# A grouped-norm and depthwise-convolution kernel: coefficients by block copies instead of a matrix product, and the last images' projections, copies and x-additions at other places

## The reference

```python
x = x + conv(gn(x), w1, w3, w5, w_proj)            # x: (8, 32, 64, 64) float32
# gn: 32 groups of one channel: each channel of each image is normalised over its 64 x 64 pixels
# conv:
xd = concatenate([x[:, :, 0::2, 0::2], x[:, :, 0::2, 1::2],
                  x[:, :, 1::2, 0::2], x[:, :, 1::2, 1::2]], axis=1)      # (8, 128, 32, 32)
feats = concatenate([dwconv(xd, w1, 1), dwconv(xd, w3, 3), dwconv(xd, w5, 5)], axis=1)
y = einsum('bchw,oc->bohw', feats, w_proj)          # 384 -> 128 channels, back to 32 x 64 x 64
```

## Time and profile before

| | us |
|---|---|
| median of 3 runs (135.26 to 136.7) | 135.5 |
| the profiled execution | 135.7 |
| its span, first to last instruction | 133.9 |
| TensorE clock granted, mean over the span | 0.986 of full |
| PE / DVE / POOL / ACT busy | 124.9 / 125.0 / 119.9 / 110.3 |

### The profile page before, as it was taken

One profiled execution on the slowest core, in us unless ns is written; L12 is line 12 of the kernel. 1 busy time (PEld: TensorE's weight loads), 2 busy tenths in 40 slices (PEclk: granted clock), 3 DMA queues, 4 the chain that ended last, 5 costly groups with the idle time before them and its releaser, 6 DMA issues.

```text
span 133.9 us, 1668 instructions
## 1 busy us (share of the span) xinstructions
PE 124.9 (93%) x514; PEld 96.8 (72%) x514; DVE 125.0 (93%) x234; ACT 110.3 (82%) x116; POOL 119.9 (90%) x92
## 2 busy tenths in 40 slices
PE   6968999999999999999999999999999999999910
PEld 6955788888886887688886888688877688578700
DVE  6679999999979999999999999999999999999960
ACT  2389979999999999999999999999999999160010
POOL 6269879999999999999999999999999999999970
PEclk9999999999999999999999999999999999999995
DMA  4999999880044008097979873989299919897876
GB/s 136 260 250 201 207 209 201 169 167 0 5 81 81 0 0 161 5 117 95 187 115 117 155 168 39 91 144 190 30 100 134 186 37 115 91 110 145 182 159 143
DMA packets 35944, 16.68 MB, mean 125 GB/s; under 512 B 34144, under 2 KB 34272, under 8 KB 35552
## 3 DMA queue, kind: packets, MB, share of 16 engines
q0 software_dynamic: 1488, 6.93, 38.8%
q1 hardware_dynamic: 32784, 9.11, 35.6%
q10 hardware_dynamic: 1664, 0.54, 1.7%
HBM read 5.46 MB, written 4.19 MB: 72 GB/s over the span
## 4 chain that ended last, share of the span: by engine, by line
POOL 62%; issue 16%; DVE 12%; PE 4%; POOLq 1%; ACT 1%; ACTq 0%
POOL RING_SUM L343 56%; DVE ACC L649 4%; POOL X L393 3%; PE YP L691 3%; POOL LO L330 2%; DVE st L546 2%; DVE weff L600 2%; DVE whi L608 1%; POOLq L102 1%; DVE ACC L645 1%; DVE stp L552 1%; DVE HI L623 1%; PE YP L795 1%; POOL rstd L312 0%; POOL wlo L385 0%
## 5 line engine op out<-in xcount | busy, mean ns | idle before, releaser
L343 POOL TENSOR_TENSOR RING_SUM<-RING_SUM,PROD 128x900 f32<-128x900 f32 (+1 forms) x45 | 93.0, 2072 | 3.4
L649 DVE SCALAR_TENSOR_TENSOR ACC<-G,coef,ACC 128x480 f32<-128x480 f32 (+3 forms) x132 | 82.4, 742 | 0.0
L476 ACT ACTIVATE PROD<-G,coef 128x900 f32<-128x900 f32 (+1 forms) x45 | 44.5, 1051 | 0.0
L723 PE MATMUL YP<-HI,wlo 128*128 128x512 f32 (+1 forms) x146 | 38.1, 412 | 0.0
L723 PE MATMUL YP<-HI,whi 128*128 128x512 f32 (+1 forms) x146 | 36.2, 398 | 1.7 <-DVE HI L623 1.2
L723 PE MATMUL YP<-LO,whi 128*128 128x512 f32 (+1 forms) x146 | 36.0, 398 | 0.0
L723 PEld LDWEIGHTS YP<-HI,wlo 128*128 128x128 f32 x146 | 27.5, 189 | 8.6 <-issue 2.9
L723 PEld LDWEIGHTS YP<-HI,whi 128*128 128x128 f32 x146 | 27.2, 189 | 8.7 <-DVE HI L623 1.3
L723 PEld LDWEIGHTS YP<-LO,whi 128*128 128x128 f32 x146 | 27.5, 189 | 6.7 <-issue 0.5
L438 ACT ACTIVATE G<-X,nbias,rstd 64x1024 f32<-64x1024 f32 x16 | 21.1, 1321 | 1.2 <-DVE nbias L564 0.9
L459 ACT ACTIVATE Y<-YP 64x1024 f32<-64x1024 f32 x14 | 15.4, 1097 | 3.4 <-PE YP L778 3.1
(11 more groups left out here) (69 smaller groups left out, 66.4 us busy)
## 6 DMA issues: line engine op xcount, KB each, us to landing
LO<-G POOLq DMA_DIRECT2D x7, 527.5 KB, 5.3
X<-in_x_dram SPq DMA_DIRECT2D x14, 256.0 KB, 5.5
X<-Y POOLq DMA_DIRECT2D x6, 512.0 KB, 7.3
out_dram<-X SPq DMA_DIRECT2D x12, 256.0 KB, 4.5
XS<-in_x_dram SPq DMA_DIRECT2D x1, 512.0 KB, 6.1
out_dram<-X SPq DMA_DIRECT2D x4, 128.0 KB, 2.2
X<-in_x_dram SPq DMA_DIRECT2D x2, 136.0 KB, 4.4
XS<-in_x_dram SPq DMA_DIRECT2D x1, 256.0 KB, 3.3
```

The lines of the kernel that those rows point to most:

```text
L343: pool.tensor_tensor(dst, dst, prod(b, k), ALU.add).then_inc(prod_added, 1)
L476: act.activation(prod(b, k), g_tap(b, POOL_OF[b][k + 1]), ACT.Copy, scale=of5(POOL_OF[b][k + 1])).then_inc(prod_ready, 1)
L649: dve.scalar_tensor_tensor(half_part(ACC, tap, h), half_tap(b, tap, h), of5(tap), half_part(ACC, tap, h), ALU.mult, ALU.add).then_inc(acc_ ...
L723: mm = nc.tensor.matmul(dst, w[:, n, :], src, start=start, stop=False, skip_group_check=True)
```

## The change

Three things at the start. The coefficients are no longer made on PE: four copies of 32 partitions each bring `w_sb` into the ph order, for w5 and w3 on DVE and for w1 on POOL, each with a semaphore of its own (`coef5`, `coef3`, `coef1`). The third part of w_proj is transposed first, ahead of the statistics' sum, into another bank and with its own count. And ACT starts seven of the weff, without a break, POOL two; PE's first row of warm matmuls has 17 for 20.

At the other end, the ring of image 4 is projected behind `low(5)`, Y of images 4 and 5 is copied inside images 6 and 7 (before products 4 and 3), the x-addition of image 4 is issued inside image 6, and x of the upper half of image 6 is added by a DMA (behind POOL's sum (7, 5)) in place of a POOL instruction. Of the lower half's two stores one is issued by ACT.

```diff
@@ -48,11 +48,11 @@
 TOP = BANK_ROWS + 1
-WARM = (20, 5)
+WARM = (17, 5)
 WARM_COLS = 256
...
 CHUNKS = N_INNER // CHUNK
-ACT_SCALED = 5
+ACT_SCALED = 7
 PARTS = 4
@@ -61,10 +61,13 @@
 AREAS = 3
-ADD_X_AT = {(b + AREAS, 0): b for b in range(B - AREAS)}
+ADD_X_AT = {(b + AREAS, 0): b for b in range(4)}
+ADD_X_AT[(6, 3)] = 4
 ADD_X_AT[(7, 1)] = 5
-COPY_Y_AT = {(7, 4): 5}
-RING_AFTER_HIGH = {2: 0, 3: 1, 4: 2, 5: 3, 6: 4, 7: 6}
+ADD_TOP6_AT = (7, 5)
+COPY_Y_AT = {(6, 4): 4, (7, 3): 5}
+RING_AFTER_HIGH = {2: 0, 3: 1, 4: 2, 5: 3, 7: 6}
+RING_AFTER_LOW = {5: 4}
 COMBINE_AT = {(0, 8): (1, 1, 2), (1, 1): (2, 2, PAIRS)}
...
@@ -244,6 +246,11 @@
+
+        def in_order(c0, c1, block):
+
+            src = (block % 2) * 2 + block // 2
+            return coef[C * block:C * (block + 1), c0:c1], w_sb[C * src:C * (src + 1), c0:c1]
@@ -269,9 +276,10 @@
                 store(b, 0, PH)
-            for half in range(2):
-                sp.wait_ge(half_added, half + 1)
-                store(B - 2, half * BANK_ROWS, (half + 1) * BANK_ROWS)
+            sp.wait_ge(row_added[B - 2], 16)
+            store(B - 2, 0, BANK_ROWS)
+            sp.wait_ge(half_added, 1)
+            store_rows(sp, B - 2, 0, BANK_ROWS, PH)
             for n, (r0, r1) in enumerate(LAST_ROWS):
@@ -343,28 +351,39 @@
                         add_x(ADD_X_AT[b, k])
+                    if (b, k) == ADD_TOP6_AT:
+                        add_x(B - 2, BANK_ROWS)
                     if (b, k) in INV_STD_AT:
...
-            def add_x(b):
+            def add_x(b, rows=PH):
...
                 pool.wait_ge(y_copied, 2 * (b + 1))
-                pool.dma_start(X[p0:p0 + HALF, t, :, :].rearrange("p h w -> p (h w)"),
-                               Y[p0:p0 + HALF, t % 2, :, :, :].rearrange("p h w j -> p (h w j)"),
+                pool.dma_start(X[p0:p0 + HALF, t, 0:rows, :].rearrange("p h w -> p (h w)"),
+                               Y[p0:p0 + HALF, t % 2, 0:rows, :, :].rearrange("p h w j -> p (h w j)"),
                                accum_op=ALU.add).then_inc(row_added[b], 16)
...
+            pool.wait_ge(wpT_ready, 1)
+            pool.wait_ge(coef5, 4)
+            scale_w5(ACT_SCALED)
             inv_std(1, 0, 1)
-            pool.wait_ge(wpT_ready, 1)
-            pool.wait_ge(coef_copied, 1)
-            scale_w5(ACT_SCALED)
             pool.wait_ge(weff_step, CHUNK)
...
                 scale_w5(n)
+            pool.wait_ge(w1_loaded, 16)
+            for block in range(PARTS):
+                if block == 0:
+                    pool.wait_ge(pool_scaled, N_INNER - ACT_SCALED)
+                else:
+                    pool.wait_ge(coef1, block)
+                to, of = in_order(W1_AT, N_COEF, block)
+                pool.tensor_copy(to, of).then_inc(coef1, 1)
+            pool.wait_ge(coef1, PARTS)
             for k in range(CHUNKS):
@@ -386,11 +405,9 @@
             pool.wait_ge(y_copied, 2 * (B - 1))
-            for half in range(2):
-                rows = slice(half * BANK_ROWS, (half + 1) * BANK_ROWS)
-                xr = X[0:HALF, PAIRS - 1, rows, :].rearrange("p h w -> p (h w)")
-                yr = Y[0:HALF, (PAIRS - 1) % 2, rows, :, :].rearrange("p h w j -> p (h w j)")
-                pool.tensor_tensor(xr, xr, yr, ALU.add).then_inc(half_added, 1)
+            xr = X[0:HALF, PAIRS - 1, BANK_ROWS:PH, :].rearrange("p h w -> p (h w)")
+            yr = Y[0:HALF, (PAIRS - 1) % 2, BANK_ROWS:PH, :, :].rearrange("p h w j -> p (h w j)")
+            pool.tensor_tensor(xr, xr, yr, ALU.add).then_inc(half_added, 1)
             pool.wait_ge(quarter_copied, 2)
...
@@ -409,18 +426,16 @@
             act.wait_ge(wt_ready, 1)
-            act.activation(wpT[:, :], WT_PS[:, 2 * P:3 * P], ACT.Copy).then_inc(wpT_ready, 1)
-            act.wait_ge(coef_ready, 1)
-            act.activation(coef[:, 0:W1_AT], COEF_PS[:, 0:W1_AT], ACT.Copy).then_inc(coef_copied, 1)
+            act.activation(wpT[:, :], SMALL[:, 0:P], ACT.Copy).then_inc(wpT_ready, 1)
             act.wait_ge(wpT_ready, 1)
-            act.wait_ge(coef_copied, 1)
+            act.wait_ge(coef5, 4)
...
-            scale_w5(0, CHUNK)
+            scale_w5(0, ACT_SCALED)
@@ -489,16 +504,13 @@
             high_half(0, TOP, 0, hi_top)
-            scale_w5(CHUNK, ACT_SCALED)
-            act.wait_ge(coef_ready, 2)
-            act.activation(coef[:, W1_AT:N_COEF], COEF_PS[:, W1_AT:N_COEF], ACT.Copy).then_inc(coef_copied, 1)
             act.wait_ge(image_loaded[0], 32)
...
             for b in range(B):
-                if b >= AREAS:
+                if AREAS <= b < B - 1:
                     copy_y(b - AREAS)
@@ -513,6 +525,8 @@
                                ACT.Copy).then_inc(quarter_copied, 1)
+            act.wait_ge(half_added, 1)
+            store_rows(act, B - 2, 1, BANK_ROWS, PH)
             for n, (r0, r1) in enumerate(LAST_ROWS):
@@ -612,22 +626,31 @@
                               mask[:, :, None].to_broadcast([P, PARTS, STATS]), ALU.mult).then_inc(spread_done, 1)
+            dve.wait_ge(w5_loaded, 16)
+            for block in range(PARTS):
+                to, of = in_order(0, W3_AT, block)
+                dve.tensor_copy(to, of).then_inc(coef5, 1)
+            dve.wait_ge(w3_loaded, 16)
+            for block in range(PARTS):
+                to, of = in_order(W3_AT, W1_AT, block)
+                dve.tensor_copy(to, of).then_inc(coef3, 1)
+            dve.wait_ge(wt_ready, 2)
+            dve.wait_ge(coef3, PARTS)
+            add_w3(0, 1)
             part_variance(0)
-            dve.wait_ge(wt_ready, 1)
-            dve.wait_ge(coef_copied, 1)
+            add_w3(2, 3)
             part_bias(0)
-            add_w3(0, 1, 2)
             dve.wait_ge(stats_ready, 1)
...
                               rstd[0:HALF, 0:1], nbias[0:HALF, 0:1], ALU.mult, ALU.add).then_inc(hi_top, 1)
-            add_w3(3, 4, 5)
+            add_w3(4, 5)
             cast_w(1)
...
             dve.wait_ge(weff_step, N_INNER)
-            dve.wait_ge(coef_copied, 2)
+            dve.wait_ge(coef1, PARTS)
             dve.scalar_tensor_tensor(weff[:, N_INNER - 1, :], transposed(0), coef[:, W1_AT:W1_AT + 1],
@@ -694,9 +717,10 @@
-            def coefficients(c0, c1):
-                nc.tensor.matmul(COEF_PS[:, c0:c1], ident_ph[:, :], w_sb[:, c0:c1],
-                                 start=True, stop=True).then_inc(coef_ready, 1)
+            def transpose(k, dst):
+
+                pe.wait_ge(permuted, 3 - k)
+                return nc.tensor.transpose(dst, wp_ph[:, k, :], ident_ph[:, :])
@@ -788,23 +812,19 @@
+            pe.wait_ge(ident_permuted, 1)
+            transpose(2, SMALL[:, 0:P]).then_inc(wt_ready, 1)
             sum_parts(0)
-            pe.wait_ge(ident_permuted, 1)
-            for n, k in enumerate((2, 1, 0)):
-                pe.wait_ge(permuted, n + 1)
-                mm = nc.tensor.transpose(WT_PS[:, k * P:(k + 1) * P], wp_ph[:, k, :], ident_ph[:, :])
-            mm.then_inc(wt_ready, 1)
-            pe.wait_ge(w_loaded, 32)
-            coefficients(0, W1_AT)
+            transpose(1, WT_PS[:, P:2 * P])
+            transpose(0, WT_PS[:, 0:P]).then_inc(wt_ready, 1)
             pe.wait_ge(low_zero, 2)
...
                 keep_warm(512)
-            pe.wait_ge(w1_loaded, 16)
-            pe.wait_ge(coef_copied, 1)
-            coefficients(W1_AT, N_COEF)
             for b in range(B):
...
                 low(b)
+                if b in RING_AFTER_LOW:
+                    ring(RING_AFTER_LOW[b])
             last_ring()
```

More of the change, by code:

```diff
@@ L152, in build @@
         WT_PS, SMALL = YP[:, 2, 0:512], YP[:, 2, 512:1024]
-        COEF_PS = SMALL[:, 200:200 + N_COEF]
         SPREAD_PS = [YP[:, 1, 512 * n:512 * n + PARTS * STATS] for n in range(2)]
@@ L160, in build @@
         xs_loaded = [sem(f"xs_loaded{n}") for n in range(3)]
-        wp_loaded, w_loaded, w1_loaded = sem("wp_loaded"), sem("w_loaded"), sem("w1_loaded")
-        coef_ready, coef_copied = sem("coef_ready"), sem("coef_copied")
+        wp_loaded, w5_loaded, w3_loaded, w1_loaded = sem("wp_loaded"), sem("w5_loaded"), sem("w3_loaded"), sem("w1_loaded")
+        coef5, coef3, coef1 = sem("coef5"), sem("coef3"), sem("coef1")
         stat_const, part_stats, spread_done = sem("stat_const"), sem("part_stats"), sem("spread_done")
@@ L186, in build @@
         half_added, last_added, stored = sem("half_added"), sem("last_added"), sem("stored")
-        row_added = [sem(f"row_added{b}") for b in range(B - 2)]
+        row_added = [sem(f"row_added{b}") for b in range(B - 1)]
         def image(tile, b, at, rows):
@@ L401, in _ @@
             load_parts(act, 0, 512, 1024, xs_loaded[1])
-            act.dma_start(w_sb[:, 0:W3_AT], w5.rearrange("c a h w -> c (a h w)")).then_inc(w_loaded, 16)
-            act.dma_start(w_sb[:, W3_AT:W1_AT], w3.rearrange("c a h w -> c (a h w)")).then_inc(w_loaded, 16)
+            act.dma_start(w_sb[:, 0:W3_AT], w5.rearrange("c a h w -> c (a h w)")).then_inc(w5_loaded, 16)
```

(1 more changed line is left out.)

## The result

The changed kernel takes 137.12 us (median of 4, 136.47 to 138.45), the kernel before on the same chip 135.5. The ratio is 1.0107, 95% interval 1.0057 to 1.0157: slower by 1.5 us. The forecast was 133.9, its range 132.9 to 135.3. The profiled execution took 137.06, its span is 135.3 (before 133.9).

A forecast was written before the change was run, and what follows sets the result against it. DVE was taken to set the middle, POOL's two additions and SP's six issues the end; 1.3 us off the tail and 0.3 off the head made 1.6, giving 133.9 against the median 135.5, range 132.9 to 135.3.

The forecast's parts named there:

- The tail: End of the kernel: one POOL addition less and stores issued earlier, 1.3 us off.
- The landing: New half DMA, image 6: lands 4.3 us after issue, between 2.65 (half the LO DMA's 5.3) and 7.3.
- third rival: SP's store queue takes the gain if the DMA lands late; chance 0.15 for 0.3 to 1.2 off, 0.05 none or slower.
- SP's last issue: Tail: the last store is issued at 129.9, 1.4 us before the former 131.3.
- this crowding I put at 0.1: Tail: about 1 MB still to be written from 125.9 on costs 0.1 us.
- The head: Start of the kernel: reordered weight preparation lets DVE's first ring tap start at 14.3 for 14.64, 0.3 us off.
- Small copies: Head, DVE: eight copies at 0.10 us each, 0.8 in all, ending before the transposes DVE must await anyway.
- the cover: Tail: POOL's sums end at 124.4, still 0.8 us before DVE's last F at 125.19, so F does not wait.
- the blocked cast: Head: DVE's second cast stays long, 1.13 us beside a POOL subtraction, where its twin lasted 0.49.
- PE must follow within its 0.3 us: Head: PE starts 0.15 to 0.2 later, waits about 0.4 less for whi, so gains 0.2 to 0.3.
- from 15 to 125 us there is next to no wait: Middle: DVE sets the pace, PE 0.3 us and POOL 1.5 us behind; time shortens only before or after it.
- Rival 4: PE's clock falls at the start in 1.7 us of idle time; 13 slow matmuls, 0.7 us slower, 136.2; chance 0.05.

The follow-up runs named there:

- E3: The changed kernel with 13 warm matmuls for 5 in the second row, filling PE's gap; 136.25 us, ratio 1.0022.
- E7: The changed kernel with image 0's variance and bias early again and 12 warm matmuls for 5 in the second row; 135.79 us, ratio 1.0001.
- E5: The kernel before with 9 warm matmuls for 5 in the second row; 135.51 us, ratio 0.9982.
- E8: The changed kernel with early variance and bias, 12 warm matmuls for 5 in the second row, and the old end; 135.57 us, ratio 0.999.
- E12: The kernel before with its second row of five warm matmuls left out, nothing else changed; 136.75 us, ratio 1.0073.
- E6: The kernel before with the new end and 9 warm matmuls for 5 in the second row; 135.55 us, ratio 0.9968.
- E2: The kernel before with the new end, its start untouched; 135.79 us, ratio 1.0006.
- E10: The kernel before with 9 warm matmuls for 5 and four tiny memsets more at POOL's start; 135.71 us, ratio 0.9994.

## Why the prediction was wrong

**The tail: -1.3 forecast, 0 measured.** POOL did as predicted: the second addition is gone and its sum is not late. Two terms failed. The landing was put at 4.3 us, nearer to the LO row; it took 5.0. From the forecast's issue at 121.6 that is 126.6, the start of the third rival's span; with the head's delay it became 127.8. Of the 1.4 us forecast for SP's last issue about 0.7 came, counted from the last F. And the step "this crowding I put at 0.1" was mis-sized by what was left: the last stores land 0.4 to 0.5 later behind their issues at the median, and the very last about 0.8. The working followed SP's issues, 0.60 each, from the earlier trace rows, and asked when the last could start; it never asked how long the bytes behind them take. 1 MB at the 200 GB/s of the windows takes 5 us, and in the new order it can start only when the half DMA has landed. The windows of before show 202 and 232 GB/s from 130 to 132 us: the row of issues looked like the bound, but the bytes were about as late. Rival 3 named the queue, but as a row of issues too; its outcome came by rate.

**The head: -0.3 forecast, about +1.6 measured.** By the medians 137.12, 136.25 (E3), 135.79 (E7) and 135.51 (E5, old head, its gap filled), this splits into 0.9 for the clock, 0.5 for the late bias, and 0.3 for what is left; by the ratios, which allow for the kernel before on the same chip, into 1.15, 0.3 and 0.25. Only the clock's part stands clear of the intervals. What is left is about what POOL's stall takes of the first F, 0.35; that the two are the same is not shown.
- The third part first: right, wpT at 5.91 for 5.9.
- Small copies: 0.10 each forecast, 0.19 to 0.23 measured (0.77 and 0.90 for four), the upper end. The first weff pair starts at 7.31 for 6.8, nbias at 9.15 for 8.85.
- The first cast shortened (0.36) and the second stayed long, 1.12 beside POOL's subtraction: as forecast, the cover and the blocked cast are right; the first ring tap came at 14.71, for 14.3, as G came 0.45 late behind the late bias.
- "PE must follow within its 0.3 us ... it gains 0.2 to 0.3": this is the step that failed most. PE's idle time was 2.59 us, not 1.7, since the warm rows ended at 7.8 for 8.3 and the first matmul came at 10.41 for 10.0, and the clock fell.
- The step under all of this, that from 15 to 125 us there is next to no wait and DVE's first ring tap sets the rest, had a hole. The rows of waits that it read, begin at 110 us. Near 37 us DVE waits for POOL already in the kernel before:

```profile
DVE nbias L587 <- POOL rstd L312: 0.7, 1, 0.7
```

Time won at the first tap is spent there in good part (E8, above), and a delay on POOL comes through it. Had the forecast's 0.3 come at the tap, it would probably not all have reached the end.

- Rival 4 had the mechanism, at over twice the price: it reckoned with 13 matmuls at the lower level, 2.6 us less 0.3 of slack. About eight of the first pass ran so, until 13.4, and the price was near 1 us. At wlo's start PE is 0.9 us behind, 0.6 of it by its late start, the rest by the clock beyond the waits for whi that it swallowed. It had a chance of 0.05 because the one profiled execution had stood 1.25 us of idle time. That was one execution; 24 of 105 of the same kernel, by their mean clocks, did not hold it.

The Trainium skill (TensorE: Matmul & The Clock Gate, "What's actually happening") calls the lower rate the default that activity releases, and says that the same kernel meets the change at another place from run to run. Both are borne out here, the first by E3 and E12, the second by the two groups of executions of the kernel before. Neither tells how likely a fall was; the two groups do.

No version run here clearly beats the kernel before. The lowest ratio of a complete one is E6's, 0.9968 (0.9936 to 0.9999); what it and E5 seem to gain over the kernel before is the share of executions in which its clock falls.

## What to carry to other kernels

Where a tail ends in stores, add up the bytes that are still to be written and divide by the rate in the windows before counting issues: the later of the two is the bound. Look for the waits of the engine that seems to set the pace over the whole stretch that it is said to set, not at its end alone. Here a warm-up row belongs right ahead of the first real matmul, and every change that makes its data later, or trims the row, must refill the gap; one profiled execution in which the clock held says little of the others, the mean clocks of all the runs say more. VectorE's small copies here cost their number, not their elements.

## What the hardware showed that was not expected

- A copy of 32 partitions by 25 or 9 elements on DVE took 0.19 to 0.23 us where 128x128 took 0.23.
- The granted clock fell to 0.50 behind 1.28 us of idle time in E2 and held behind 1.25 in the profiled execution of before; once down it stayed so for over 3 us (from 10.0 until past 13, in E12 the same).
- A cast on DVE that started 0.15 us ahead of a POOL subtraction took 0.40 us (E8), one that started 0.08 behind it 1.14 (E7).
- A DMA that adds 256 KB landed in 5.0 us, one of 512 KB in 7.3 at the median: half the bytes, two thirds of the time.
- POOL stood for 0.5 us between two instructions of one loop in every kernel in which instructions had been added ahead of it (E10, and all with the new head), and in none with the old head. Why is open.
